# Issuing the constant loads together and moving the bias broadcast behind the first LayerNorm tile

## The reference

```python
def reference(x, wq, wk, wv, wo, weight, bias):      # x [8, 2048, 2048], weights [2048, 2048]
    xn = layernorm(x)
    q, k, v = xn @ wq, xn @ wk, xn @ wv              # 16 heads of 128
    q, k = rope(q), rope(k)
    attn = softmax(q @ k.T / sqrt(128) + causal_mask)   # per head
    a = (attn @ v).reshape(...) @ wo
    scale = mean(abs(weight))
    w_t = clip(round(weight / (scale + 1e-10)), -1, 1) * scale
    return x + a + xn @ w_t.T + bias
```

## Time and profile before

| | |
|---|---|
| median of 2 runs | 1915.93 us (1906.36 and 1925.51) |
| profiled execution, time | 1916.98 us |
| its span (slowest core, 3) | 1915.4 us |
| spans of all cores | 1860.0 to 1915.4 us |
| PE busy | 1542.5 us, 81% of the span |
| DVE, ACT, POOL busy | 724.5, 540.7, 101.2 us |
| DMA | 194.94 MB, mean 102 GB/s |

### The profile page before, as it was taken

How to read it: one execution, slowest core, us unless ns; L and a number is a source line. 1 busy time by engine, 2 the same in 40 slices (tenths; PEclk the granted TensorE clock), 3 DMA queues, 4 the chain that set the end, 5 groups by cost and what they waited for, 6 DMA issues and landing times. The chain is left out here.

```text
span 1915.4 us, 29654 instructions; the slowest of 8 cores (1860.0 to 1915.4 us)
## 1 busy us (share of the span) xinstructions
PE 1542.5 (81%) x9096; PEld 886.3 (46%) x9096; DVE 724.5 (38%) x1527; ACT 540.7 (28%) x901; POOL 101.2 (5%) x117
## 2 busy tenths in 40 slices
PE   0134349999999899999999999999278999898989
PEld 0011114344444344444444444444067878787878
DVE  0142234345435357457447447445011222122212
ACT  2232144563463442451452452353200000000000
POOL 0100001011010100000000000000000000000000
PEclk9977579999999999999999999999688999999999
DMA  3985945056156673573573463300737474647462
GB/s 117 168 142 62 95 68 109 26 108 123 59 105 97 115 131 75 86 127 78 85 131 79 85 106 60 45 7 12 188 103 145 113 152 111 152 113 155 115 151 73
DMA packets 350391, 194.94 MB, mean 102 GB/s; under 512 B 240163, under 2 KB 338468, under 8 KB 343844
## 3 DMA queue, kind: packets, MB, share of 16 engines
q0 software_dynamic: 139040, 92.29, 29.6%
q1 hardware_dynamic: 190756, 80.31, 21.3%
q10 hardware_dynamic: 20448, 20.46, 3.2%
HBM read 177.28 MB, written 32.51 MB: 110 GB/s over the span
## 5 line engine op out<-in xcount | busy, mean ns | idle before, releaser
L599 ACT ACTIVATE et<-pC,bias 128x512 bf16<-128x512 f32 (+3 forms) x240 | 149.9, 625 | 610.6 <-PE pC L586 610.2
L636 PE MATMUL pF<-et,onms 128*128 128x512 bf16 (+3 forms) x640 | 222.9, 350 | 17.9 <-ACT et L599 12.3
L950 PE MATMUL pA<-woc,oTh 128*128 128x256 bf16 x896 | 121.5, 293 | 88.6 <-DVE osl L980 51.6
L496 PE MATMUL pB<-xnT,wslv 128*128 128x512 bf16 x480 | 115.2, 395 | 85.8 <-DVE prawk L511 85.8
L496 PE MATMUL pA<-xnT,wslk 128*128 128x512 bf16 x480 | 115.9, 397 | 83.1 <-DMA xnT<-xnn 83.0
L610 DVE TENSOR_TENSOR et<-et,trim 128x128 bf16<-128x128 bf16 x256 | 56.9, 225 | 267.2 <-ACT et L599 264.1
L977 DVE TENSOR_TENSOR osl<-pA,xsl 128x256 f32<-128x256 f32 x64 | 27.2, 425 | 313.1 <-PE pA L957 165.4
L950 PEld LDWEIGHTS pA<-woc,oTh 128*128 128x128 bf16 x896 | 92.4, 104 | 108.0 <-issue 92.5
L638 PE MATMUL pG<-et,vh 128*128 128x512 bf16 (+3 forms) x384 | 135.3, 356 | 0.0
L599 ACT ACTIVATE et<-pD,bias 128x512 bf16<-128x512 f32 (+3 forms) x208 | 130.8, 629 | 1.5 <-PE pD L586 1.0
L586 PE MATMUL pC<-qTh,kTh 128*128 128x512 bf16 (+3 forms) x240 | 83.4, 348 | 56.2 <-ACT et L599 56.2
(11 more groups left out here) (97 smaller groups left out, 1985.4 us busy)
## 6 DMA issues: line engine op xcount, KB each, us to landing
xst<-wf POOLq DMA_DIRECT2D x32, 1024.0 KB, 7.3
xst<-x POOLq DMA_DIRECT2D x16, 1024.0 KB, 16.5
woc<-wo POOLq DMA_DIRECT2D x16, 1024.0 KB, 12.5
wtc<-wtT_scr SPq DMA_DIRECT2D x16, 1024.0 KB, 6.4
xsl<-x SPq DMA_DIRECT2D x128, 128.0 KB, 3.6
y<-osl ACTq DMA_DIRECT2D x128, 128.0 KB, 3.5
wslq<-wq POOLq DMA_DIRECT2D x16, 512.0 KB, 8.3
wslk<-wk POOLq DMA_DIRECT2D x16, 512.0 KB, 10.1
```

The source lines that it names most:

```text
L496: e.matmul(pp[:, 0:CW], wsl[:, it * 128:(it + 1) * 128], bass.AP(xnT, it * S + c * CW, [[NT * S, 128], [1, CW]]), start=(it == 0), stop=False)
L599: e.activation(out=et[slot][:, col0:CW], in_=pc_[:, col0:CW], func=AF.Exp, scale=INV_SQRT_D, bias=bias3[:, :]).then_inc(sems["ac"], 1)
L636: e.matmul(pF[:, col0:CW], onm[:, :], et[slot][:, col0:CW], start=(kt == 0), stop=(kt == nkt - 1))
L950: e.matmul(pp[:, 0:W2], lh, woc[ecb][:, it * W2:(it + 1) * W2], start=(it == 0), stop=False)
```

## The change

The helper `dma` gets a switch, `ordered`. With `ordered=False` a load doesn't wait for the one before on its semaphore; the eight constant loads use it. All the same every reader of constants waits for the full count of eight loads.

The bias broadcast is taken apart. PE writes the first three quarters into pH, pE and pG, with no wait between them. The three copies on ACT, the fourth matmul (into pH, after the first copy) and its copy are moved behind the instructions of LayerNorm tile 0: on ACT they stand between tile 0 and tile 1, on PE ahead of the first projection. The first score block that is written to pH waits for the fourth copy. DVE's wait for the copies in the second part takes its count from where the copies are planned now.

```diff
--- before.py
+++ after.py
@@ -133,8 +133,8 @@
             cnt[name] += amt
             return cnt[name]
 
-        def dma(engname, sem_name, make_out_in, extra_waits=()):
-            prev = cnt[sem_name]
+        def dma(engname, sem_name, make_out_in, extra_waits=(), ordered=True):
+            prev = cnt[sem_name] if ordered else 0
             ws = tuple(extra_waits)
 
             @on(engname)
@@ -153,7 +153,8 @@
 
         for dst, src in [(c2, c2_d), (s2, s2_d), (tri, tri_d), (onc, onc_d),
                          (oncf, oncf_d), (onr, onr_d), (onrf, onrf_d), (onm, onm_d)]:
-            dma("sync", "c", (lambda dst=dst, src=src: (dst[:, :], src, False)))
+            dma("sync", "c", (lambda dst=dst, src=src: (dst[:, :], src, False)),
+                ordered=False)
         consts_c = cnt["c"]
         dma("gpsimd", "bias", (lambda: (biasb[:, :], bias_d, False)))
         bias_v = cnt["bias"]
@@ -164,26 +165,45 @@
             e.memset(bias3[:, :], -3.0)
             e.wait_ge(sems["c"], consts_c)
 
-        prev_bb_ac = 0
-        for j in range(4):
+        bb_banks = [pH, pE, pG, pH]
+        bb_pe = [0] * 4
+        for j in range(3):
             @on("tensor")
-            def _(e, j=j, bv=bias_v, pba=prev_bb_ac):
+            def _(e, j=j, bv=bias_v, bk=bb_banks[j]):
                 if j == 0:
                     e.wait_ge(sems["c"], consts_c)
                     e.wait_ge(sems["bias"], bv)
-                else:
-                    e.wait_ge(sems["ac"], pba)
-                e.matmul(pH[:, 0:512], onr[:, :], biasb[0:1, j * 512:(j + 1) * 512],
+                e.matmul(bk[:, 0:512], onr[:, :], biasb[0:1, j * 512:(j + 1) * 512],
                          start=True, stop=True).then_inc(sems["pe"], 1)
-            pe_bb = bump("pe")
+            bb_pe[j] = bump("pe")
+        bb_state = {"biasbc_ac": 0, "pH_gate": 0}
+
+        def plan_bias_copies():
+            copy_acs = [0] * 4
+            for j in range(3):
+                @on("scalar")
+                def _(e, j=j, pe_bb=bb_pe[j]):
+                    e.wait_ge(sems["pe"], pe_bb)
+                    e.activation(out=biasbc[:, j * 512:(j + 1) * 512],
+                                 in_=bb_banks[j][:, 0:512],
+                                 func=AF.Copy).then_inc(sems["ac"], 1)
+                copy_acs[j] = bump("ac")
+
+            @on("tensor")
+            def _(e, c0=copy_acs[0]):
+                e.wait_ge(sems["ac"], c0)
+                e.matmul(pH[:, 0:512], onr[:, :], biasb[0:1, 3 * 512:4 * 512],
+                         start=True, stop=True).then_inc(sems["pe"], 1)
+            bb_pe[3] = bump("pe")
 
             @on("scalar")
-            def _(e, j=j, pe_bb=pe_bb):
+            def _(e, pe_bb=bb_pe[3]):
                 e.wait_ge(sems["pe"], pe_bb)
-                e.activation(out=biasbc[:, j * 512:(j + 1) * 512], in_=pH[:, 0:512],
+                e.activation(out=biasbc[:, 3 * 512:4 * 512], in_=pH[:, 0:512],
                              func=AF.Copy).then_inc(sems["ac"], 1)
-            prev_bb_ac = bump("ac")
-        biasbc_ac = cnt["ac"]
+            copy_acs[3] = bump("ac")
+            bb_state["biasbc_ac"] = copy_acs[3]
+            bb_state["pH_gate"] = copy_acs[3]
 
         @on("tensor")
         def _(e):
@@ -276,7 +296,9 @@
                                   xnn[b2][:, :], True)),
                               extra_waits=[("dv", dv_xn)]))
 
-        for tt in range(4):
+        plan_ln_tile(0)
+        plan_bias_copies()
+        for tt in range(1, 4):
             plan_ln_tile(tt)
         xnT_ready = 16 * (NT // 2)
 
@@ -576,6 +598,9 @@
                     n = CW - col0
                     pc_ = sc_psums[sc_state["parity"]]
                     my_free = sc_free_ac[sc_state["parity"]]
+                    if my_free == 0 and pc_ is pH and bb_state["pH_gate"]:
+                        my_free = bb_state["pH_gate"]
+                        bb_state["pH_gate"] = 0
 
                     @on("tensor")
                     def _(e, pc_=pc_, kt=kt, col0=col0, n=n, my_free=my_free,
@@ -968,7 +993,7 @@
                     @on("vector")
                     def _(e, pp=pp, tb=tb, ec=ec, xsp=xsp, syp=syp, pe_out=pe_out,
                           xsl_ld=xsl_ld, osl_gate=osl_st[tb], dv_out1=dv_out1,
-                          bac=biasbc_ac):
+                          bac=bb_state["biasbc_ac"]):
                         e.wait_ge(sems["pe"], pe_out)
                         e.wait_ge(sems[xsp], xsl_ld)
                         e.wait_ge(sems["ac"], bac)
```

## The result

| | before | after |
|---|---|---|
| median of the runs beside each other | 1921.46 us (10 runs, 1906.36 to 1937.0) | 1895.94 us (11 runs) |
| ratio, 95% interval | | 0.9849 (0.9809 to 0.9889) |
| profiled execution, its span | 1916.98, 1915.4 us | 1898.05, 1896.5 us |
| mean over the eight cores, kept runs | 1887.6 us | 1868.9 us |
| slowest core, the same runs | 1919.6 us | 1893.6 us |

Both intervals exclude no change, and both lie under the 2% that the prediction took for the size that can be told from no change. Runs in which one half of the chip ran at a lower clock, or which took over 1.5% longer than the fastest of the same kernel, are left out of every mean and ratio here, but not of the medians.

The account below looks back on a forecast made before the run. Matmuls bound 300 to 1300 us; before that a start-up chain without overlap sets the first transpose. Gain 21.7 - 0.5 = 21.2 us: profiled 1917.0 to 1895.8, predicted 1895, range 1880 to 1914 (forecast's own 1887 to 1900).

Parts of the forecast that it names:

- Constants: SP's eight constant loads, issued without waiting, all landed at 20.5 us instead of 31.3, bounds 17.3 and 22.5.
- T0: Issue of the first transpose, after LayerNorm tile 0: forecast at 23.5 us instead of 45.2, so 21.7 earlier.
- x tile 0: First input load: lands at 14.4 us instead of 11.4 through sharing with the second table; bounds 11.4 and 20.9.
- The copies: Four bias copies on ACT between LayerNorm tiles 0 and 1: 2.4 us long, costing 0 to 0.9, taken as 0.5.
- rival C: Weight loads gain a lead over tile 1's transpose and core 3's setback grows: slower than before, 1945 us; chance 0.06.
- What hangs on T0: Claim that all later transposes, loads and projections on core 3 follow the first transpose, nothing being tied to another moment.
- the way marks: First projection at 69 us on core 3 and 61 on core 0; last projections and end earlier by the same 21.
- A: Start-up queues: x tile 0 lands only with the third x tile, gain 14.9 us, time 1901; chance 0.15.
- B: From 90 to 300 us the slowest core meets 10 to 20 us more sharing, time 1905 to 1915; chance 0.16.
- D: Every core behaves like core 0, so faster by more, about 1841 us; chance 0.07.
- E: Constants still land at 31.3 us, only the reordering counts, gain 10.9 - 0.5, time 1906; chance 0.04.

Follow-up runs that it names:

- e4: Changed kernel with DVE's constants wait moved to its first rotation and both rotary tables issued behind tile 1's transpose; ratio to the kernel before 0.984.
- the halves: Kernel before with only the unordered constant loads, ratio 0.989; changed kernel with ordered loads again, so only the moved bias copies, ratio 0.994.
- the delay run: Changed kernel with seven useless DVE copies, 10 us planned, ahead of DVE's first LayerNorm step; ratio to the kernel before 1.007.
- e5: The changed kernel measured again, unchanged, against the kernel before; ratio 0.989, mean of the cores 21.4 us lower.
- e9: Changed kernel with head 1's weight loads, and x loads behind them, held until the first four transposes are over; ratio to the kernel before 0.998.
- e10: Changed kernel with bias rounds through one bank and head 1's weight loads held until the first four transposes landed; ratio to the kernel before 0.997.
- e12: Last version: changed kernel, late tables, DVE's wait at first rotation, x tiles 4-6 ahead of head 1's weights, both held; ratio to the kernel before 0.990.

## Why the prediction was right

**Size and sign.** Forecast were 1895 us and 21 us gained; measured were 1895.94 us and 18.7 and 21.4 us on the mean of the cores, 26 and 21 on the slowest one. The mechanism and the size came out, but the agreement of the time within 1 us is luck: the kernel before, taken as 1915.9, had a median of 1921.46 beside the changed one, and the changed kernel itself had 1904.79 when measured again.

**Constants.** Taken as 20.5, between 17.3 and 22.5; it was 21.55, with the last issued at 4.5 to 4.9 us and not by 4. The upper bound was nearer, but not only because x kept the engines full (DMA share 0.84 in 0 to 20 us). By 12 us SP's queue, q1, had moved 2.10 of its 2.16 MB, nearly all of the tables. What came last were the six small constants: their packets ran one for one with x's, so they moved next to nothing until x was through. Core 5, 12 to 18 us (queue, packets, MB, share):

```profile
q0 software_dynamic: 260, 1.87, 93.5%
q1 hardware_dynamic: 260, 0.03, 3.5%
```

That the small loads, and not the tables, end the wait is what the prediction didn't see; e4, without the tables, had them at 13.2 to 14.7 us, still after x tile 0 (8.7 us on core 5). One bound was also worked out wrong: with the constants at 17.3 DVE would have waited for ACT until 19.9, so T0 could be earlier by 22.3 us at most and not by 24.9, by the prediction's own terms.

**x tile 0.** Its landing was put at 14.4 for sharing with the second table; ACT started at 14.27, where before the load had landed at 11.4. The bytes of the two queues show the sharing. Up to 8.2 us:

```profile
q1 hardware_dynamic: 220, 1.67, 68.7%
q0 software_dynamic: 41, 0.09, 4.8%
```

and from 8.4 to 12:

```profile
q0 software_dynamic: 85, 0.70, 60.8%
q1 hardware_dynamic: 78, 0.39, 32.2%
```

From 8.4 to 12 the packets are 85 and 78, where q0 had all 145 before. Up to 8.2 they are 41 and 220. q0 starts later, its first packets on core 5 fall in 5 to 6 us in both kernels, but before the change it had 84 packets up to 8.2 us on this core, so the sharing begins before 8.4, where the prediction let it begin. And it ends sooner: from 12 us on q1's packets are tiny and x has the engines nearly to itself. The two misses cancel, so the 14.4 is in part luck. The rule that the prediction cites from the Trainium skill, DMA: Bandwidth & Descriptors, section Queues, rings and completion order, that each engine goes round the queue rows packet by packet, fits 85 to 78 and above all 260 to 260.

**T0.** 23.5 was forecast, 24.5 measured, the miss being the constants' 1.0. That DVE would wait for the constants and not for ACT was right, by 1.9 us (19.67, 21.55); the run without that wait showed that 1.7 of them could be had and were worth nothing that the measurement can tell. Adding up the halves, 9.0 + 11.0 = 20.0, confirms the sum.

**The copies.** 2.4 us were forecast and 2.04 measured, since one activation begins before the last has ended. Their cost of 0.5 is not told apart from none. But my reason was incomplete: a later transpose of tile 1 is not only hidden behind tile 0's, it also lets the weight loads ahead, and that is rival C's mechanism. With the 2 us of the three banks it doesn't show; with the 5 of one bank it set the even cores back by 8.6 us at the projection and the end by 6 ± 3 (-15.6 ± 1.8 beside -21.4 ± 2.3; straight from the two means 5.8 ± 2.4). It never came near the 21 from which C decides.

**What hangs on T0.** I wrote that nothing is tied to another moment. The whole change and the delay run support it for a shift of everything: 18.7 and 21.4 us at the end for 19.8 and 19.5 at T0, and 10.7 ± 2.3 (or 16 to 18) for 8.5 to 8.8. The halves gave less, 7.8 ± 1.9 for 9.0 and 6.2 ± 1.8 for 11.0, so the factor is near one and not known closely. It fails where only a part moves. The late tables, the held weights and the last version all moved the first projection by 8 to 14 us and the attention not at all or the wrong way. That the transfers behind T0 are a fixed sum which only changes its order is how I read this; the rows of core 3 fit it, and no run tried it by itself. The forecast for the way marks shows it in small: on core 0 the projection came at 65.2, not 61, on core 3 at 72.1, not 69, and over all cores it gained 18.3 of T0's 19.8 (16.4 of 19.5 in e5). The last key projection was to be 21 earlier and was so by 22.2 on core 0 and 36.9 on core 3.

**The rivals.** A had its delay (11.4 to 14.3) but it was hidden behind the constants. B, sharing between the cores, took nothing that can be told: attention gained 17.7 and 17.0, the end 18.7 and 21.4. D and E didn't occur. The 26 us of the first comparison looked like a little of D, and the second measurement took it back.

## What to carry to other kernels

A start-up chain of waits is worth what it delays: sum its steps, compare with what the transfers need anyway, and the rest is the gain, if all that follows moves as one piece. Once the transfers behind it are dense, moving a single one only changes which of them is late; the mark to watch is then not the first matmul but the first that needs the last of these transfers. In e9, e10 and e12 the first projection came 27 to 30 us earlier than before, the first attention 12 to 15 and the end 12 to 15. Even that mark is rough: with one bank the attention came 9.1 us later than in e5 and the end only 5.8 ± 2.4. And where readers wait for a group of loads, look at which of them comes last, not only at the sum of the bytes: here the six small constants were there only when the x tiles were through. Where a measurement of the slowest core scatters by more than the gain, the mean over the cores and a second measurement tell the size.

## What the runs showed of the hardware

In these runs transposes by DMA are slower beside ordinary loads than I had allowed for. With the loads held back, the first projection, which waits for the first four transposes, came 12 us earlier (70.0 to 58.1) with the first issue at 24.4 and not 25.0; with the same x loads issued earlier, beside the transposes, it came 12 us later (82.2). Whether the engines' queues or the memory set this is not shown.

The even cores were ahead of the odd ones at the first attention in every kernel but the one-bank one (127.2 and 142.6 in the changed kernel; 148.8 and 139.1 there), and the order turned over with a shift of 3 us in one activation, each in one profiled execution. What makes even and odd cores differ wasn't tried.
